# Two expert routers of a transformer block on one NeuronCore: the turned rows become the stationary operand, the router's columns move

## What is computed

```
# layer 0: 8 experts, the 2 best by raw score
logits = xf @ router_w.T                       # [1600, 256] x [256, 8]
top_vals, top_idx = jax.lax.top_k(logits, TOPK)
top_w = jax.nn.softmax(top_vals, axis=-1)
...
# layer 1: 16 experts in 4 groups, the 2 best groups, in them the 2 best experts
scores = jax.nn.sigmoid(xf @ gate_w.T)         # [1600, 256] x [256, 16]
group_scores = jax.lax.top_k(sg, min(2, gs))[0].sum(axis=-1)
...
out = shared                                   # silu(xf @ sw1) @ sw2
for e in range(E):
    out = out + combine[:, e:e + 1] * (jax.nn.silu(xf @ w1[e]) @ w2[e])
```

## Time and profile before

| | |
|---|---|
| median of 3 timed runs | 1830.09 us |
| lowest and highest of them | 1828.99 and 1832.86 us |
| the profiled execution, its own time | 1837.43 us |
| its span, first to last instruction | 1835.6 us |
| mean granted TensorE clock | 0.931 |
| TensorE busy | 1633.0 us, 89% of the span |
| VectorE, GpSimd, ScalarE busy | 67%, 50%, 40% of the span |

### The profile page before, as it was taken

How to read it: one execution, slowest core, us unless ns; L and a number is a source line. 1 busy time by engine, 2 the same in 40 slices (tenths; PEclk the granted TensorE clock), 3 DMA queues, 4 the chain that set the end, 5 groups by cost and what they waited for, 6 DMA issues and landing times. The chain is left out here.

```text
span 1835.6 us, 27630 instructions
## 1 busy us (share of the span) xinstructions
PE 1633.0 (89%) x8770; PEld 1115.5 (61%) x8770; DVE 1230.1 (67%) x2197; ACT 742.1 (40%) x1964; POOL 920.1 (50%) x799
## 2 busy tenths in 40 slices
PE   5999977999999999999999996799999389978880
PEld 3677744555555555555555563599998367655780
DVE  5598768777778777777777734566665766655433
ACT  3100102444444444444444442466665166632220
POOL 0377747777788877777778550133332000000636
PEclk9999987999999999999999997599999599978895
DMA  6434344122221222122221004544443610000343
GB/s 197 132 69 94 72 118 117 42 78 78 78 78 41 74 78 70 57 72 78 78 78 38 10 11 160 206 144 129 139 140 89 181 26 0 0 26 15 119 112 107
DMA packets 91472, 157.41 MB, mean 86 GB/s; under 512 B 45841, under 2 KB 70645, under 8 KB 88077
## 3 DMA queue, kind: packets, MB, share of 16 engines
q1 hardware_dynamic: 84301, 138.86, 25.6%
q0 software_dynamic: 7040, 16.92, 3.4%
HBM read 125.31 MB, written 28.48 MB: 84 GB/s over the span
## 5 line engine op out<-in xcount | busy, mean ns | idle before, releaser
L897 ACT ACTIVATE R<-banks 128x400 f32<-128x400 f32 x768 | 326.6, 510 | 318.2 <-PE banks L931 317.4
L713 DVE TENSOR_REDUCE PM<-banks 128x2 f32<-128x964 f32 x320 | 360.9, 1133 | 137.5 <-PE banks L690 137.5
L751 POOL TENSOR_TENSOR EA<-EA,R 128x400 f32<-128x400 f32 x288 | 306.6, 1064 | 119.0 <-ACT R L897 105.6
L931 PE MATMUL banks<-QS,KH 128*128 128x400 f32 x768 | 288.9, 376 | 2.5 <-DMA QB<-ML 2.5
L931 PE MATMUL banks<-QB,KB 128*128 128x400 f32 x768 | 265.6, 346 | 0.0
L731 DVE TENSOR_TENSOR banks<-banks,R 128x400 f32<-128x400 f32 x320 | 183.8, 574 | 27.9 <-ACT R L897 26.7
L540 POOL TENSOR_TENSOR arena<-arena 96x400 f32<-96x400 f32 x128 | 141.3, 1123 | 116.6 <-DVE arena L515 116.4
L941 PE MATMUL banks<-R,KV 128*64 128x400 f32 x960 | 187.5, 512 | 0.0
L931 PEld LDWEIGHTS banks<-QS,KH 128*128 128x128 f32 x768 | 145.2, 189 | 54.5 <-issue 38.4
L690 PE MATMUL banks<-KH,QS 64*128 64x482 f32 x320 | 160.5, 502 | 17.2 <-DVE PM L713 7.7
L690 PEld LDWEIGHTS banks<-KH,QS 64*128 64x128 f32 x320 | 60.7, 190 | 160.6 <-DVE PM L713 86.6
(11 more groups left out here) (287 smaller groups left out, 3251.2 us busy)
## 6 DMA issues: line engine op xcount, KB each, us to landing
arena<-in_ctx_T SPq DMA_DIRECT2D x16, 1444.0 KB
m_stage_d<-in_m_down SPq DMA_DIRECT2D x32, 672.0 KB
QS<-queries SPq DMA_DIRECT2D x16, 800.0 KB, 6.6
m_up<-in_m_up SPq DMA_DIRECT2D x8, 1392.0 KB, 13.0
queries<-q_out_h SPq DMA_DIRECT2D x64, 100.0 KB, 2.4
queries<-q_out_l SPq DMA_DIRECT2D x64, 100.0 KB, 2.4
QB<-queries SPq DMA_DIRECT2D x16, 400.0 KB, 8.2
arena<-recips SPq DMA_DIRECT2D x32, 200.0 KB
```

The source lines that it names most:

```text
L713: nc.vector.tensor_reduce(PM[:, 2 * i:2 * i + n], banks[:, k:k + n, 0:KW], AX.X, ALU.max).then_inc(red_done, 1)
L751: nc.gpsimd.tensor_tensor(out, first, tile_of(n, 1), ALU.add).then_inc(odd_sum, 1)
L897: nc.scalar.activation(tile_of(n, o), psum[ring_bank(score_tile(b, n, o))][:, 0:CH], ACT.Exp).then_inc(exp_done, 1)
L931: last = nc.tensor.matmul(out, lhs[r][:, keys], heads[:, o], start=lhs is KH, stop=lhs is KB)
```

## The change

The operands of the routers' product change places. For each sequence and each half of the features, the 128x100 piece of `XT` is loaded as the stationary operand and the router's 8 or 16 columns move; the result has tokens on partitions and goes straight to its place in bank LOG. `flat`, its copies on ScalarE, `upright` and two semaphores are gone. The accumulation starts once for the whole bank (`start` on the first matmul alone). Turns, copies to `XT` and all that follows the scores stay as they were. Lines behind the edit move up: the product is L1184, the turn L1175, keys L2072, values L2081, `shared_up` L1808.

```
-        def across(c):
+        def scores(c):
             pe.wait_ge(self.xt_act, c + 1)
             pe.wait_ge(self.xt_dve, c + 1)
-            if c >= 2:
-                pe.wait_ge(self.flat_in, c - 1)
-            for k in range(KD):
-                last = nc.tensor.matmul(psum[self.RANK + c % 2][0:E, 0:CH], self.router[:, k, :],
-                                        self.XT[:, k, c * CH:(c + 1) * CH], start=k == 0, stop=k == KD - 1)
-            last.then_inc(self.flat_ready, 1)
-
-        def upright(c):
-            pe.wait_ge(self.flat_in, c + 1)
             for b in range(c * CB, (c + 1) * CB):
-                last = nc.tensor.transpose(psum[self.LOG][0:S, b * E:(b + 1) * E], self.flat[:, b * S:(b + 1) * S], self.ident[0:E, 0:E])
+                for k in range(KD):
+                    last = nc.tensor.matmul(psum[self.LOG][0:S, b * E:(b + 1) * E], self.XT[:, k, b * S:(b + 1) * S],
+                                            self.router[:, k, :], start=b == 0 and k == 0, stop=b == B - 1 and k == KD - 1)
             if c == NC - 1:
                 last.then_inc(self.scores, 1)
...
         for c in range(NC):
-            across(c)
+            scores(c)
             if c + 2 < NC:
                 turn(c + 2)
-            if c:
-                upright(c - 1)
-        upright(NC - 1)
...
-        for c in range(NC + 1):
-            if c < NC:
-                n = c * KD
-                act.wait_ge(self.turned, n + 1)
-                nc.scalar.activation(self.XT[:, 0, c * CH:(c + 1) * CH], psum[3 + n % 5][:, 0:CH], ACT.Copy).then_inc(self.xt_act, 1)
-            if c:
-                act.wait_ge(self.flat_ready, c)
-                nc.scalar.activation(self.flat[:, (c - 1) * CH:c * CH], psum[self.RANK + (c - 1) % 2][0:self.E, 0:CH],
-                                     ACT.Copy).then_inc(self.flat_in, 1)
+        for c in range(NC):
+            n = c * KD
+            act.wait_ge(self.turned, n + 1)
+            nc.scalar.activation(self.XT[:, 0, c * CH:(c + 1) * CH], psum[3 + n % 5][:, 0:CH], ACT.Copy).then_inc(self.xt_act, 1)
```

More of the change, by code:

```diff
@@ L1084, in __init__ @@
         self.small = fixed(stage, nc, tag + "small", [S, 8, B])
-        self.flat = fixed(stage, nc, tag + "flat", [E, B * S])
         self.trib = fixed(stage, nc, tag + "trib", [S, S], BF16)
@@ L1125, in __init__ @@
         self.xt_dve = core.sem(tag + "xt_dve")
-        self.flat_ready = core.sem(tag + "flat")
-        self.flat_in = core.sem(tag + "flat_in")
         self.scores = core.sem(tag + "scores")
```

## The result

The changed kernel takes 1841.28 us (median of 20 runs) against 1832.65 us for the kernel before on the same chips: a ratio of 1.0047, 95% interval 1.0039 to 1.0056, or 7.1 to 10.3 us more. The change makes the kernel slower, as forecast, but by more: I had said 1836.0 us, 1830.5 to 1840.5.

A forecast was written before the change was run, and what follows sets the result against it. Near each router engines wait for one another, so the ranks' start sets the block's end. Router 1's +3.25, router 2's +2.1 and 0.5 for clock variation, given as 5.9 us, on 1830.09 made 1836.0 us; range 1830.5 to 1840.5.

The forecast's parts named there:

- The clock stays low through the scores and the keys: Router 1: the granted clock stays at 0.50 (1.2 GHz) through the new score rows and ten key rows.
- Rival A: Both routers: weight loads count, the clock rises where it did; -1.5 and about -2.5 us, 1826.1 us; chance 0.10.
- 0.167 us a row at the low clock, 13.75 us for the scores, keys 6.7 us: Router 1: 64 score rows at 0.167 us, scores 13.75 us in all, ten key rows 6.7 us instead of 3.5.
- Ranks of router 1 +3.25 us: Router 1: TensorE becomes later than VectorE ahead of the ranks, so ranks and block end come 3.25 us later.
- rival B: Both routers: scores run low but only VectorE's path counts; +1.8 and +1.75 us, 1833.6 us; chance 0.08.
- Ranks of router 2 +2.1 us: Router 2: ranks +1.9 to +2.7 us, taken as +2.1, the clock rising 4.2 to 6.0 us into the shared expert.
- the race that I gave to TensorE: Router 2, ahead of the ranks: TensorE's shared expert ends at 1670.4 to 1671.2, after VectorE's `both` at 1670.2.
- Rival C: Router 2: the clock doesn't rise on the shared expert or after; +16 us in router 2, 1849 us; chance 0.04.
- the term for the kernel before: Router 1 before the change: an earlier clock rise would make it 0.9 us faster; half, 0.5, was added.

The follow-up runs named there:

- e6: The changed kernel with four extra matmuls, results unused, in each router: 1842.89 us, ratio 1.0029 against the kernel before.
- e4: The changed kernel with 96 moving columns in each score product instead of 8 or 16: 1823.97 us, ratio 0.9950 against the kernel before.
- e9: The changed kernel with 96 moving columns per score product, measured a second time: 1833.89 us, ratio 0.9968 against the kernel before.
- e10: The changed kernel without a further edit, measured a third time: 1844.96 us, ratio 1.0040 against the kernel before.
- e3: The kernel before with only router 2 changed, router 1 as before: 1835.71 us, ratio 1.0016 against the kernel before.
- e8: The kernel before, run and traced again without an edit: 1836.41 us, ratio 0.9992.
- e5: The kernel before with four extra matmuls, results unused, in each router: 1833.06 us, ratio 0.9970 against the kernel before.

## Why the prediction was right in kind and short in size

**The clock stays low through the scores and the keys:** right, in every trace of the changed router 1. Rival A (loads hold or raise the clock) is refuted by 13.3 us of unbroken work at 0.50 and by e6. The Trainium skill ("TensorE: Matmul & The Clock Gate", "Part 1: The HAM clock gate") says that the gate follows how busy TensorE has recently been. Read as occupancy this doesn't agree with the traces, which show PE and PEld busy for 13.3 of 13.3 us at 0.50. That the width of the stream made the difference here is shown by e4 and e9.

**0.167 us a row at the low clock, 13.75 us for the scores, keys 6.7 us:** right; 0.164, 13.4 and 7.03. By the Trainium skill ("TensorE: Matmul & The Clock Gate", section "LDWEIGHTS (loading the stationary operand)") a load of 100 columns is 83 ns, as an estimate. That agrees with 0.087 us a row at the high clock and is half of what a row costs here at the low one.

**Ranks of router 1 +3.25 us against the profiled execution:** right, +3.36, and rival B, in which VectorE stays the late one, is refuted: its `both` was there 1.9 us before.

**Ranks of router 2 +2.1 us:** +1.45 in the first pair, +1.9 to +2.3 for the block over all traces. In the first pair the clock rose after 3.4 us of the shared expert, sooner than the 4.2 to 6.0 I had (3.4 to 4.6 in the four traces of the changed router 2 without extra matmuls). So the race that I gave to TensorE was a tie there: VectorE's path, +1.47, is the whole delay of the ranks, as rival B has it for this router, and TensorE was late by 0.3 to 0.4 us in e10 and e3. The block grew by 1.87 us, more than its ranks, because the clock falls 2.7 us ahead of its last 32 rows (1683.55 and 1686.27), where the first trace has them start 0.3 us before the fall; the list rows and the 32 rows run low, 3.19 and 13.95 us instead of 2.93 and 13.76. Rival C did not occur; its +16 us is 14.7 by the two terms that it names, 7.9 and 6.8.

**The step that failed** is the term for the kernel before: "had router 1's come after 4.2 us as router 2's did, the kernel before would be 1.8 x 0.5 = 0.9 us faster there", of which I took half. In the traces it is 2.5 us. I priced only the rise, and only the rows ahead of the ranks, 0.6 us in e8. I left out the fall: with it 2 us later behind the first product, the ranks and the first of the six key rows run under the high clock too, and that is 1.9 of the 2.5 us (e8). And I took the profiled execution as the usual one, with half a microsecond as correction, although its own time, 1837.43, was 7.3 us above the median. Against a router 1 of 42.20 us the change costs 5.9 us there; with 2 us in router 2 that is 7.9, against 6.4, 7.3 and 8.6 measured. Against one of 44.71 us it is 5.4. That the shorter router 1 is the usual one fits these times, but the traces are too few to show it.

The forecast of 1836.0 us missed by 5.3. Of this 2.7 us lie in the cost of the change, 8.6 instead of 5.9, by the step above. The other 2.6 us lie in the starting point: the kernel before had a median of 1832.65 us in 20 runs and 1830.09 in the three that I was shown. Either alone would have left the measured time within the range.

What stays open: how often the shorter router 1 occurs (e8 and e3, and e5 with its extra matmuls, against the first trace), what moves the rise and the fall between executions, and what of e4's gain is real.

## What to carry to other kernels

Swapping the operands of this thin product is even in TensorE's time at one clock. But the clock rose behind the streams of 400 columns and stayed up for the keys, and behind 8 or 16 columns with a 100-column load it didn't rise. Before removing the only long stream of a stretch, price the rows that follow at the low clock too. If the load bounds the row anyway, try more moving columns: 96 instead of 8 cost 0.15 us in 16 rows here. And where the clock rises inside the stretch that is changed, read more than one trace: where it rises and falls is part of the price.

## What I had not expected of the hardware

Matmuls from 88 of the array's 128 rows ran at either clock. In the changed kernel two groups of 32 such rows show it:

```profile
1674.41 7.15 PE L1819 MATMUL banks<-m_down,s_hidden 88*100 88x256 f32 x32 [0.59 <-ACT s_hidden L1842]
...
1686.27 13.95 PE L1819 MATMUL banks<-m_down,s_hidden 88*100 88x256 f32 x32
```

The first group, behind rows from 128 of the array's rows, stays at 1.00 to its end. The second, behind the lists, stays at 0.50 for 13.95 us without a gap and never wins the clock. The fp32 transposes take 0.17 us each at the low clock and about 0.1 at the high one (eight in 0.91 us). And one change can leave the profiled spans equal (1835.6 and 1835.1 us) where 20 runs differ by 8.6 us.
